# Rounding work given to GpSimd and weight loads to SyncE's queue, in a two-layer model on eight cores

## The chip, the cores and the metric

The kernel runs on all 8 cores of one Trainium2 chip. Each core computes one sequence of a batch of 8, with all weights; the cores exchange nothing. The metric is the device time of the slowest core, in microseconds (us).

## The reference

Two layers with layer norms behind every block, on x of [8, 2048, 1024]. Cut to what matters:

```python
# layer 0
x = _layernorm(x + _L0_attn_ref(x, ...))   # k, v, sigmoid(r); a scan over time; Wo
x = _layernorm(x + _L0_ffn_ref(x, ...))    # 1024 -> 4096 -> 4096 -> 4096 -> 1024
# layer 1: every linear layer is quantized
x = _layernorm(x + _L1_attn_ref(x, ...))
x = _layernorm(x + _L1_ffn_ref(x, ...))    # 1024 -> 4096, conv over 3 tokens, silu, 4096 -> 1024

def act_quant(x):       # per token
    scale = 127.0 / clip(max(abs(x), axis=-1), 1e-05)
    return clip(round(x * scale), -128.0, 127.0) / scale
def weight_quant(w):    # per matrix
    scale = 1.0 / clip(mean(abs(w)), 1e-05)
    return clip(round(w * scale), -1.0, 1.0) / scale
def bitlinear(x, norm_w, w, b=None):
    return act_quant(rmsnorm(x, norm_w)) @ weight_quant(w).T
def _L1_attn_ref(x, ...):
    q, k, v, g = bitlinear(x, nq, wq), ...            # 1024, 1024, 2048, 2048 wide
    gk = log_sigmoid(bitlinear(bitlinear(x, ngk1, wgk1), ngk2, wgk2, bgk2)) / 16
    # S = exp(gk_t) S + k_t v_t ; o_t = q_t S, per head, over time
    return bitlinear(o * silu(g), no, wo)
```

## The kernel before

Five engines run in parallel: TensorE (PE, "t" in the code), VectorE (DVE, "v"), ScalarE (ACT, "s"), GpSimd (POOL, "g") and SyncE (SP, "y"). `Prog` keeps one list of instructions for each. `P.op(engine, fn, after=...)` appends a computation that waits on the semaphores of the tokens in `after`, its own engine's too; `P.dma(queue, out, in_, after=..., new=True)` appends a DMA to the list of the engine that issues it. Each engine executes its list strictly in order. So an instruction's place in the program decides what it stands behind, and a DMA issued by POOL stands behind all that POOL has to do before it.

The work goes through eight stages on activations XA that stay in SBUF: first attention, LN 1, first feed-forward, LN 2, layer 1's attention, LN 3, layer 1's feed-forward, LN 4.

**Weight prepass** (`_emit_prepass`). Layer 1's nine weight matrices are made ternary beforehand and written to DRAM. A matrix is cut in tiles of 128x1024 fp32 (512 KB): 137 tiles in all, 32 of them of f1T, 32 of f2T, 16 of owT. Every tile passes twice. In `t_red` it is loaded, ACT sums its absolute values into `red` (L393), and POOL adds that to `acc` (L397). After the matrix's last tile comes its scale: a matmul on PE (L403) and an op on DVE (L406). In `t_quant` it is loaded again, DVE turns it to -1, 0 or 1 in three ops (L425, L428, L431: v1, v2, v4), and POOL stores it, in eight DMAs for a tile of f1T or f2T and one for the others. These pieces (301 in all) stand in a list `P.bg`. `P.pump(1)` calls in the first attention (96) and in LN 1 (16) put one each between the stage's instructions, and `P.pump_all()` after LN 1 puts all the rest there, before the first feed-forward.

**Layer 1's attention** (`stage_l1attn`) runs over 8 blocks of 256 tokens. In a block X2 holds two token tiles (tt) of 128 x 1024. For each of the five projections in NPROJ (q, k, v, g, gk1) and each of the two tiles, DVE multiplies by the norm vector NB (p1, L973), takes the maximum (p2, L977), computes four columns of scales in `CL` (p3 to p6), and rounds in seven ops q1 to q7 (L991 to L1005): scale, cast to int32, cast back, difference, two comparisons that correct the rounding, and unscale. The tensors are QSz, QSi, QSt, QSd. PE transposes the tile in eight matmuls (L1014) into banks 5 and 6, DVE evacuates them into XQF (L1019), and the projection's matmuls (L1057 or L1076) read XQF and the weights WL, a single buffer of 2 MB that a DMA on POOL's queue fills. Then a chunked scan over time (L1157 to L1262) yields OG for each of two halves `cn` of the block. OG is quantized in two halves of 1024 (L1311 to L1324, y1 to y8, eight ops each, the same kind as p1 and q1 to q7), transposed, and multiplied with owT, which comes in two loads (`rnd`) into WL.

**Layer 1's feed-forward** (`stage_l1ffn`) runs over four quarters of 512 tokens. Each of four token tiles is transposed, copied to QZ, scaled and rounded by seven ops like q1 to q7 (L1499 to L1508), and transposed back into XQ3. 32 output slices with f1T follow, then the convolution, then `_act_quant_fm` (L1386 to L1409), which rounds HC (128 x 16384) in 16 pieces of 1024, eight ops each, then 8 slices with f2T. Weights come through three buffers FWJ on POOL's queue, each load after the matmuls that read its buffer last.

In both stages one token `vt` threads all of DVE's ops.

## Time and profile before

| | us |
|---|---|
| median of 3 runs | 12935.47 (12914.56 to 12952.62) |
| the profiled execution, its own time | 12926.71 |
| its span, first to last instruction, on the slowest core | 12925.1 |
| spans of the 8 cores | 12856.7 to 12925.1 |
| busy: PE, weight loads, DVE | 5345.3, 2561.2, 3718.3 |
| busy: ACT, POOL | 1284.4, 908.4 |

The profiled execution's time is 8.8 us below the median and 1.6 us above its own span. A stage by stage table of the trace is the way to read this profile, since no engine is busy throughout: the whole-span shares mix stages with different limits. The first attention ends near 890 us, LN 1 near 1,126, the drained prepass near 2,510, the first feed-forward near 6,915, LN 2 near 7,075, layer 1's attention near 10,600, LN 3 near 10,756, layer 1's feed-forward near 12,770. Of POOL's instructions nearly all are DMA issues; the rest are adds and memsets of one column.

### The profile page before, as it was taken

Reading aid. Unit: us, or ns where it says so; the run is one execution under the profiler, and the core shown is the slowest. Engines: PE = TensorE matmul, PEld = TensorE weight load, DVE = VectorE, ACT = ScalarE, POOL = GpSimd, SP = SyncE. Lnnn points to the kernel's source line nnn. Section 1 sums busy time; section 2 is a strip of 40 time slices with the busy share of each in tenths; the row PEclk is TensorE's granted clock in tenths of the full one; section 3 lists DMA queues with packets and bytes.
Section 4 is the critical chain, followed back from the end, with each engine's and each line's share of the span. In section 5 each row is a group of like instructions: output and inputs, shape, how many; then the busy total and the mean of one; then the engine's idle time right before and its main releaser. Section 6 shows DMA issues by size and latency. Waiting matters only on the chain.

```text
span 12925.1 us, 71867 instructions; the slowest of 8 cores (12856.7 to 12925.1 us)
## 1 busy us (share of the span) xinstructions
PE 5345.3 (41%) x22678; PEld 2561.2 (20%) x22678; DVE 3718.3 (29%) x6428; ACT 1284.4 (10%) x2046; POOL 908.4 (7%) x1789
## 2 busy tenths in 40 slices
PE   2431000166666666666664333333333333324323
PEld 0110000022222222222222222222221222111111
DVE  5752120210000001000002444444444434553553
ACT  1221101010000001000002100100010012011011
POOL 1011142300000000000000000000000000000000
PEclk7665555588888887888886666666666666657656
DMA  4221222222222222222221111111111101001002
GB/s 102 63 75 58 83 65 77 60 39 44 43 43 43 44 39 40 43 43 43 46 43 27 55 56 55 42 56 56 42 41 56 69 20 32 24 29 52 24 29 73
DMA packets 169413, 637.25 MB, mean 49 GB/s; under 512 B 28928, under 2 KB 29568, under 8 KB 157776
## 3 DMA queue, kind: packets, MB, share of 16 engines
q0 software_dynamic: 163136, 615.49, 18.5%
q1 hardware_dynamic: 5904, 17.17, 0.4%
q8 instruction: 187, 3.06, 0.1%
q14 instruction: 186, 1.52, 0.0%
HBM read 794.50 MB, written 42.01 MB: 65 GB/s over the span
## 4 chain that ended last, share of the span: by engine, by line
PE 37%; DVE 25%; DMA 20%; issue 8%; ACT 5%; POOL 3%; DVEq 1%; another core or an unknown queue 0%; ACTq 0%; POOLq 0%; SPq 0%
PE ps L817 16%; PE ps L769 5%; DMA f_wj<-h1R 4%; DMA f_wj<-h2R 4%; PE ps L1634 2%; DMA pre_in<-f1T 2%; PE ps L854 2%; DMA pre_in<-f2T 2%; DMA f_wj<-w1R 2%; PE ps L1076 2%; PE ps L1241 2%; PE ps L1534 2%; PE ps L1357 1%; PE ps L1057 1%; DMA b_wj<-q_f2T 1%
## 5 line engine op out<-in xcount | busy, mean ns | idle before, releaser
L817 PE MATMUL ps<-f_h,f_wj 128*128 128x512 bf16 x8192 | 2014.2, 412 | 1103.2 <-DMA f_wj<-h1R 554.3
L817 PEld LDWEIGHTS ps<-f_h,f_wj 128*128 128x128 bf16 x8192 | 855.2, 104 | 2262.3 <-issue 1471.8
L865 DVE SCALAR_TENSOR_TENSOR XA<-ps,SVEC,XA 128x512 f32<-128x512 f32 x32 | 24.0, 751 | 3478.8 <-PE ps L854 3477.1
L769 PE MATMUL ps<-f_h,f_wj 128*128 128x512 bf16 x2048 | 584.8, 456 | 690.1 <-DMA f_wj<-w1R 683.1
L1634 PE MATMUL ps<-b_hc,b_wj 128*128 128x512 bf16 x1024 | 280.1, 442 | 607.9 <-DVE b_hc L1406 466.5
L403 PE MATMUL ps<-pre_acc,c_ones 128*128 128x1 f32 x18 | 4.7, 332 | 1201.2 <-POOL pre_acc L397 1201.2
L828 ACT ACTIVATE f_h<-ps,f_sc 128x512 bf16<-128x512 f32 x256 | 175.9, 687 | 2893.6 <-PE ps L817 2881.4
L769 PEld LDWEIGHTS ps<-f_h,f_wj 128*128 128x128 bf16 x2048 | 232.0, 113 | 1042.4 <-issue 897.4
L1014 PE MATMUL ps<-c_idb,a_qz 128*128 128x128 bf16 x640 | 77.7, 298 | 766.6 <-DVE a_qz L1005 766.6
L1076 PE MATMUL ps<-a_wl,a_xqf 128*128 128x512 bf16 x1024 | 302.8, 468 | 149.9 <-DMA a_wl<-q_vwT 68.0
L789 DVE SCALAR_TENSOR_TENSOR f_h<-ps,f_sc,f_g 128x512 bf16<-128x512 f32 x128 | 96.1, 751 | 796.8 <-ACT f_g L779 790.1
L425 DVE TENSOR_SCALAR pre_in<-pre_in,pre_rs 128x1024 f32<-128x1024 f32 (+1 forms) x137 | 98.9, 722 | 771.3 <-DMA pre_in<-f1T 287.4
L854 PE MATMUL ps<-f_h,f_wj 128*128 128x512 bf16 x1024 | 251.6, 412 | 136.8 <-DMA f_wj<-w3R 136.8
L1221 PE MATMUL ps<-a_qg,a_kp 128*128 128x128 f32 x256 | 76.4, 454 | 524.9 <-DVE a_kg L1214 524.9
L1579 PE MATMUL ps<-c_idb,b_hc 128*128 128x128 bf16 x512 | 74.9, 301 | 523.9 <-ACT b_hc L1562 396.8
L393 ACT ACTIVATE pre_in<-pre_in 128x1024 f32<-128x1024 f32 (+1 forms) x137 | 138.0, 1007 | 1358.9 <-DMA pre_in<-f2T 544.0
L1634 PEld LDWEIGHTS ps<-b_hc,b_wj 128*128 128x128 bf16 x1024 | 111.0, 111 | 781.3 <-issue 698.8
L1534 PE MATMUL ps<-b_xq,b_wj 128*128 128x512 bf16 x1024 | 240.8, 387 | 15.8 <-DMA b_wj<-q_f1T 8.3
L403 PEld LDWEIGHTS ps<-pre_acc,c_ones 128*128 128x128 f32 x18 | 4.4, 298 | 1203.3 <-issue 1203.2
L1357 PE MATMUL ps<-a_oqf,a_wl 128*128 128x128 bf16 x2048 | 179.1, 273 | 152.6 <-DMA a_wl<-q_owT 139.0
L529 PE MATMUL ps<-l_xk,l_wk 128*128 128x512 bf16 x256 | 106.5, 591 | 324.5 <-DVE l_xr L515 183.0
L687 PE MATMUL ps<-c_idf,ln_tm 128*128 128x128 f32 x384 | 93.1, 423 | 310.7 <-DVE ln_tm L668 310.7
(323 smaller groups left out, 7916.2 us busy)
## 6 DMA issues: line engine op xcount, KB each, us to landing
f_wj<-h1R POOLq DMA_DIRECT2D x128, 512.0 KB, 6.4
f_wj<-h2R POOLq DMA_DIRECT2D x128, 512.0 KB, 6.2
a_wl<-q_owT POOLq DMA_DIRECT2D x32, 2048.0 KB, 7.8
b_wj<-q_f2T POOLq DMA_DIRECT2D x80, 512.0 KB, 4.6
pre_in<-f1T POOLq DMA_DIRECT2D x64, 512.0 KB, 3.9
pre_in<-f2T POOLq DMA_DIRECT2D x64, 512.0 KB, 3.8
a_wl<-q_vwT POOLq DMA_DIRECT2D x16, 2048.0 KB, 7.6
a_wl<-q_gwT POOLq DMA_DIRECT2D x16, 2048.0 KB, 7.6
```

The lines of the kernel that those rows point to most:

```text
L393: s1 = P.op("s", lambda s: s.activation(buf[0:rr, 0:cc], buf[0:rr, 0:cc], AF.Abs, accum_out=pre["red"][0:rr, :]), after=[ld, state["s"], s ...
L529: mmK = P.op("t", lambda t, c=c, i=i, bk=bk: t.matmul(PS[bk][:, :], WK[:, i, c * 128:(c + 1) * 128], XK[:, i, :], start=(i == 0), stop=(i ...
L769: t.matmul(PS[bank][:, :], wb[:, i, :], XB[:, i, s2 * 512:(s2 + 1) * 512], start=(i == 0), stop=(i == NC - 1)),
L817: off=off, SRC=SRC: t.matmul(PS[bank][:, :], wb[:, i2, :], SRC[:, i * 1024 + off:i * 1024 + off + 512], start=(i == 0), stop=(i == 31)),
L828: DST=DST: s.activation(DST[:, j * 1024 + off:j * 1024 + off + 512], PS[bank][:, :], AF.Gelu, scale=SC[:, scoff + j:scoff + j + 1]),
L854: off=off: t.matmul(PS[bank][:, :], wb[:, i2, :], H0[:, i * 1024 + off:i * 1024 + off + 512], start=(i == 0), stop=(i == 31)),
L1057: mm = P.op("t", lambda t, i=i, j=j, bank=bank: t.matmul(PS[bank][:, 0:256], WLv[:, i, j * 128:(j + 1) * 128], XQF[:, i, :], start=(i == 0 ...
L1076: t.matmul(PS[bank][:, :], XQF[:, i, tt * 128:(tt + 1) * 128], WLv[:, i, ds * 512:(ds + 1) * 512], start=(i == 0), stop=(i == NC - 1)),
L1241: omm = P.op("t", lambda t, h=h, j=j: t.matmul(PS[3][:, :], QG[:, j, :], S[:, 2 * h + j, :], start=(j == 0), stop=False), after=[f3, bank_ ...
L1357: cc=cc: t.matmul(PS[bank][:, cc * 128:(cc + 1) * 128], WLv[:, i, jj * 128:(jj + 1) * 128], OQF[:, rnd * 8 + i, :], start=(rnd == 0 and i ...
L1534: mm = P.op("t", lambda t, slot=slot, i=i, j=j, bank=bank: t.matmul(PS[bank][:, :], FWJ[slot][:, i, :], XQ3[:, i, :], start=(i == 0), stop ...
L1634: t.matmul(PS[bank][:, :], FWJ[s_][:, i2, :], HC[:, i, :], start=(i == 0), stop=(i == 31)),
```

## The change

There are two parts.

1. In the prepass, loads are issued by SP instead of POOL, into three buffers instead of two. A reduce load waits for the ACT op that read its buffer three tiles ago, no longer for POOL's last add; `red` has two buffers. A quantize load waits for the DVE op that read its buffer three tiles ago and for `state["v"]`; the wait for the earlier store moves from the load to v4. The scale's matmul uses bank 7 instead of 6.
2. In layer 1, part of the rounding runs on POOL. In the attention: of every projection the second token tile (p1, q1 to q7, not p2 to p6), and of the output quantization the second half (y1 to y8). In the feed-forward: of four token tiles the second and fourth, and of `_act_quant_fm`'s pieces every second. POOL has buffers of its own (Q2z, Q2i, Q2t, Q2d, CL2, MSKF) and its own token `gt`. Rounding goes through a new helper, `_round_fix`: on DVE five ops as before, on POOL seven, since each scalar_tensor_tensor becomes a comparison and an add. `zb_free` makes the writer of a buffer wait for the transposes that read it. The norm vector's load waits for both tiles' p1, no longer for the end of the block before.

```diff
-                buf = (pre["in0"], pre["in1"])[ti % 2]
-                ld = P.dma("g", buf[0:rr, 0:cc], src[r0:r0 + rr, c0:c0 + cc],
-                           after=[state["g"]], new=True)
+                buf = pre["ins"][ti % NR]
+                red = pre["reds"][ti % 2]
+                ld = P.dma("y", buf[0:rr, 0:cc], src[r0:r0 + rr, c0:c0 + cc],
+                           after=[state["ld"][ti % NR]], new=True)
                 s1 = P.op("s", lambda s: s.activation(
                     buf[0:rr, 0:cc], buf[0:rr, 0:cc], AF.Abs,
-                    accum_out=pre["red"][0:rr, :]), after=[ld, state["s"], state["g"]])
+                    accum_out=red[0:rr, :]), after=[ld, state["s"],
+                                                    state["redf"][ti % 2]])
                 state["s"] = s1
+                state["ld"][ti % NR] = s1
                 state["g"] = P.op("g", lambda g: g.tensor_add(
-                    pre["acc"][0:rr, :], pre["acc"][0:rr, :], pre["red"][0:rr, :]),
+                    pre["acc"][0:rr, :], pre["acc"][0:rr, :], red[0:rr, :]),
                     after=[s1, state["g"]])
+                state["redf"][ti % 2] = state["g"]
...
-                buf = (pre["in0"], pre["in1"])[ti % 2]
-                obuf = (pre["out0"], pre["out1"])[ti % 2]
-                ld = P.dma("g", buf[0:rr, 0:cc], src[r0:r0 + rr, c0:c0 + cc],
-                           after=[state["qd"][ti % 2], state["v"], state["g"]], new=True)
+                buf = pre["ins"][ti % NR]
+                obuf = pre["outs"][ti % 2]
+                ld = P.dma("y", buf[0:rr, 0:cc], src[r0:r0 + rr, c0:c0 + cc],
+                           after=[state["ld"][ti % NR], state["v"]], new=True)
                 v1 = P.op("v", lambda v: v.tensor_single_scalar(
                     buf[0:rr, 0:cc], buf[0:rr, 0:cc], pre["rs"][0:rr, :], ALU.mult),
                     after=[ld, state["v"]])
@@ -430,8 +436,9 @@
                     ALU.is_le, ALU.mult), after=[v1])
                 v4 = P.op("v", lambda v: v.scalar_tensor_tensor(
                     obuf[0:rr, 0:cc], buf[0:rr, 0:cc], 0.5, pre["cmp"][0:rr, 0:cc],
-                    ALU.is_ge, ALU.add), after=[v2])
+                    ALU.is_ge, ALU.add), after=[v2, state["qd"][ti % 2]])
                 state["v"] = v4
+                state["ld"][ti % NR] = v4
...
                 d_nb = P.dma("g", NB[:, 0:1024], din[nnm], new=True,
-                             after=[nb_free])
+                             after=[nb_free2[0], nb_free2[1]])
                 qtoks = []
                 for tt in range(2):
-                    p1 = P.op("v", lambda v, tt=tt: v.tensor_mul(
-                        QSz[:], X2[:, tt, :], NB[:, 0:1024]),
-                        after=[d_nb, x2tok, vt])
-                    nb_free = p1
-                    p2 = P.op("v", lambda v: v.reduce_max(
-                        CL[:, 4:5], QSz[:], axis=AXX, apply_absolute_value=True),
-                        after=[p1])
-                    p3 = P.op("v", lambda v, tt=tt: v.tensor_scalar(
-                        CL[:, 5:6], CL[:, 4:5], CL[:, tt:tt + 1], 1e-5,
+                    en = "v" if tt == 0 else "g"
+                    Zb, Ib, Tb, Db = (QSz, QSi, QSt, QSd) if tt == 0 else (Q2z, Q2i, Q2t, Q2d)
+                    CLx = CL if tt == 0 else CL2
+                    ch = vt if tt == 0 else gt
+                    p1 = P.op(en, lambda v, tt=tt, Zb=Zb: v.tensor_mul(
+                        Zb[:], X2[:, tt, :], NB[:, 0:1024]),
+                        after=[d_nb, x2tok, ch, zb_free[tt]])
+                    nb_free2[tt] = p1
+                    p2 = P.op("v", lambda v, Zb=Zb, CLx=CLx: v.reduce_max(
+                        CLx[:, 4:5], Zb[:], axis=AXX, apply_absolute_value=True),
+                        after=[p1, vt])
+                    p3 = P.op("v", lambda v, tt=tt, CLx=CLx: v.tensor_scalar(
+                        CLx[:, 5:6], CLx[:, 4:5], CL[:, tt:tt + 1], 1e-5,
                         ALU.mult, ALU.max), after=[p2, c3])
-                    p4 = P.op("v", lambda v: v.reciprocal(CL[:, 6:7], CL[:, 5:6]),
-                              after=[p3])
-                    p5 = P.op("v", lambda v, tt=tt: v.scalar_tensor_tensor(
-                        CL[:, 7:8], CL[:, 6:7], 127.0, CL[:, tt:tt + 1],
+                    p4 = P.op("v", lambda v, CLx=CLx: v.reciprocal(
+                        CLx[:, 6:7], CLx[:, 5:6]), after=[p3])
+                    p5 = P.op("v", lambda v, tt=tt, CLx=CLx: v.scalar_tensor_tensor(
+                        CLx[:, 7:8], CLx[:, 6:7], 127.0, CL[:, tt:tt + 1],
                         ALU.mult, ALU.mult), after=[p4])
-                    p6 = P.op("v", lambda v: v.tensor_scalar(
-                        CL[:, 8:9], CL[:, 5:6], 1.0 / 127, None, ALU.mult),
+                    p6 = P.op("v", lambda v, CLx=CLx: v.tensor_scalar(
+                        CLx[:, 8:9], CLx[:, 5:6], 1.0 / 127, None, ALU.mult),
                         after=[p5])
-                    q1 = P.op("v", lambda v: v.tensor_single_scalar(
-                        QSz[:], QSz[:], CL[:, 7:8], ALU.mult), after=[p6])
-                    q2 = P.op("v", lambda v: v.tensor_copy(QSi[:], QSz[:]),
-                              after=[q1])
-                    q3 = P.op("v", lambda v: v.tensor_copy(QSt[:], QSi[:]),
-                              after=[q2])
-                    q4 = P.op("v", lambda v: v.tensor_sub(QSd[:], QSz[:], QSt[:]),
-                              after=[q3])
-                    q5 = P.op("v", lambda v: v.scalar_tensor_tensor(
-                        QSt[:], QSd[:], 0.5, QSt[:], ALU.is_ge, ALU.add),
-                        after=[q4])
-                    q6 = P.op("v", lambda v: v.scalar_tensor_tensor(
-                        QSt[:], QSd[:], -0.5, QSt[:], ALU.is_gt, ALU.add),
-                        after=[q5])
-                    q7 = P.op("v", lambda v: v.tensor_scalar(
-                        QSz[:], QSt[:], 1.0, CL[:, 8:9], ALU.subtract, ALU.mult),
+                    if tt == 0:
+                        vt = p6
+                    q1 = P.op(en, lambda v, Zb=Zb, CLx=CLx: v.tensor_single_scalar(
+                        Zb[:], Zb[:], CLx[:, 7:8], ALU.mult), after=[p6, ch])
+                    q6 = _round_fix(P, en, Zb, Ib, Tb, Db, Zb, q1)
+                    q7 = P.op(en, lambda v, Zb=Zb, Tb=Tb, CLx=CLx: v.tensor_scalar(
+                        Zb[:], Tb[:], 1.0, CLx[:, 8:9], ALU.subtract, ALU.mult),
                         after=[q6])
-                    vt = q7
+                    if tt == 0:
+                        vt = q7
+                    else:
+                        gt = q7
                     xtp = []
                     for c in range(NC):
                         bank = 5 + c // 4
                         cc = c % 4
                         a = [q7, bank_free[bank]] if (c % 4 == 0) else []
-                        xtp.append(P.op("t", lambda t, c=c, bank=bank, cc=cc: t.transpose(
+                        xtp.append(P.op("t", lambda t, c=c, bank=bank, cc=cc, Zb=Zb:
+                                        t.transpose(
                             PSB[bank][:, cc * 128:(cc + 1) * 128],
-                            QSz[:, c * 128:(c + 1) * 128], IDB[:]), after=a))
+                            Zb[:, c * 128:(c + 1) * 128], IDB[:]), after=a))
+                    zb_free[tt] = xtp[-1]
...
+                    en = "v" if half == 0 else "g"
+                    Zb, Ib, Tb, Db = (QSz, QSi, QSt, QSd) if half == 0 else (Q2z, Q2i, Q2t, Q2d)
+                    ch = vt if half == 0 else gt
+                    y1 = P.op(en, lambda v, half=half, Zb=Zb: v.tensor_mul(
+                        Zb[:], OG[:, half * 1024:(half + 1) * 1024],
+                        NOB[:, half * 1024:(half + 1) * 1024]),
+                        after=[ch, w7, zb_free[half]])
+                    y2 = P.op(en, lambda v, Zb=Zb: v.tensor_single_scalar(
+                        Zb[:], Zb[:], CL[:, 7:8], ALU.mult), after=[y1])
+                    y7_ = _round_fix(P, en, Zb, Ib, Tb, Db, Zb, y2)
+                    y8 = P.op(en, lambda v, Zb=Zb, Tb=Tb: v.tensor_scalar(
+                        Zb[:], Tb[:], 1.0, CL[:, 8:9], ALU.subtract, ALU.mult),
+                        after=[y7_])
+                    ytoks[half] = y8
+                    if half == 0:
+                        vt = y8
+                    else:
+                        gt = y8
...
+def _round_fix(P, en, Zb, Ib, Tb, Db, M, prev):
+    o1 = P.op(en, lambda v, Zb=Zb, Ib=Ib: v.tensor_copy(Ib[:], Zb[:]), after=[prev])
+    o2 = P.op(en, lambda v, Ib=Ib, Tb=Tb: v.tensor_copy(Tb[:], Ib[:]), after=[o1])
+    o3 = P.op(en, lambda v, Zb=Zb, Tb=Tb, Db=Db: v.tensor_sub(Db[:], Zb[:], Tb[:]),
+              after=[o2])
+    if en == "v":
+        o4 = P.op(en, lambda v, Tb=Tb, Db=Db: v.scalar_tensor_tensor(
+            Tb[:], Db[:], 0.5, Tb[:], ALU.is_ge, ALU.add), after=[o3])
+        o5 = P.op(en, lambda v, Tb=Tb, Db=Db: v.scalar_tensor_tensor(
+            Tb[:], Db[:], -0.5, Tb[:], ALU.is_gt, ALU.add), after=[o4])
+    else:
+        o4a = P.op(en, lambda v, Db=Db, M=M: v.tensor_single_scalar(
+            M[:], Db[:], 0.5, ALU.is_ge), after=[o3])
+        o4 = P.op(en, lambda v, Tb=Tb, M=M: v.tensor_add(Tb[:], Tb[:], M[:]),
+                  after=[o4a])
+        o5a = P.op(en, lambda v, Db=Db, M=M: v.tensor_single_scalar(
+            M[:], Db[:], -0.5, ALU.is_gt), after=[o4])
+        o5 = P.op(en, lambda v, Tb=Tb, M=M: v.tensor_add(Tb[:], Tb[:], M[:]),
+                  after=[o5a])
+    return o5
+
+
+def _act_quant_fm(P, flat, UB, WB, QSV, QSG, vt, gt, ready=None):
     piece = 1024
     for pc in range(16384 // piece):
         o0 = pc * piece
-        q1 = P.op("v", lambda v, o0=o0: v.tensor_mul(
+        en = "v" if pc % 2 == 0 else "g"
+        QI, QT, QD, QM = QSV if pc % 2 == 0 else QSG
+        ch = vt if pc % 2 == 0 else gt
+        q1 = P.op(en, lambda v, o0=o0: v.tensor_mul(
             flat[:, o0:o0 + piece], flat[:, o0:o0 + piece], UB[:, 0:piece]),
-            after=[vt])
-        q2 = P.op("v", lambda v, o0=o0: v.tensor_copy(
-            QI[:, 0:piece], flat[:, o0:o0 + piece]), after=[q1])
-        q3 = P.op("v", lambda v: v.tensor_copy(QT[:, 0:piece], QI[:, 0:piece]),
-                  after=[q2])
-        q4 = P.op("v", lambda v, o0=o0: v.tensor_sub(
-            QD[:, 0:piece], flat[:, o0:o0 + piece], QT[:, 0:piece]), after=[q3])
-        q5 = P.op("v", lambda v: v.scalar_tensor_tensor(
-            QT[:, 0:piece], QD[:, 0:piece], 0.5, QT[:, 0:piece], ALU.is_ge, ALU.add),
-            after=[q4])
-        q6 = P.op("v", lambda v: v.scalar_tensor_tensor(
-            QT[:, 0:piece], QD[:, 0:piece], -0.5, QT[:, 0:piece], ALU.is_gt, ALU.add),
-            after=[q5])
-        q7 = P.op("v", lambda v: v.tensor_scalar(
+            after=[ch, ready if pc < 2 else None])
+        q6 = _round_fix(P, en, flat[:, o0:o0 + piece], QI[:, 0:piece],
+                        QT[:, 0:piece], QD[:, 0:piece], QM[:, 0:piece], q1)
+        q7 = P.op(en, lambda v, QT=QT: v.tensor_scalar(
             QT[:, 0:piece], QT[:, 0:piece], 1.0, None, ALU.subtract), after=[q6])
-        q8 = P.op("v", lambda v, o0=o0: v.tensor_mul(
+        q8 = P.op(en, lambda v, o0=o0, QT=QT: v.tensor_mul(
             flat[:, o0:o0 + piece], QT[:, 0:piece], WB[:, 0:piece]), after=[q7])
-        vt = q8
-    return vt
+        if pc % 2 == 0:
+            vt = q8
+        else:
+            gt = q8
+    return vt, gt
...
+                en = "v" if tt % 2 == 0 else "g"
+                Zb, Ib, Tb, Db = (QZ, QI, QT, QD) if tt % 2 == 0 else (Q2z, Q2i, Q2t, Q2d)
+                CLx = CL if tt % 2 == 0 else CL2
+                ch = vt if tt % 2 == 0 else gt
...
+                b1 = P.op(en, lambda v, Zb=Zb, CLx=CLx: v.tensor_single_scalar(
+                    Zb[:], Zb[:], CLx[:, 3:4], ALU.mult), after=[a5, ch])
+                b6 = _round_fix(P, en, Zb, Ib, Tb, Db, MSKF[tt % 2], b1)
+                b7 = P.op(en, lambda v, Zb=Zb, Tb=Tb, CLx=CLx: v.tensor_scalar(
+                    Zb[:], Tb[:], 1.0, CLx[:, 4:5], ALU.subtract, ALU.mult), after=[b6])
+                if tt % 2 == 0:
+                    vt = b7
+                else:
+                    gt = b7
...
+            vt, gt = _act_quant_fm(P, HC[:, :, :].rearrange("p c n -> p (c n)"),
+                                   UB, WB, (QI, QT, QD, MSKF[0]),
+                                   (Q2i, Q2t, Q2d, MSKF[1]), vt, gt, ready=vt)
+            hq_tok = (vt, gt)
```

## Rows read from the trace of the kernel before

**Rows 1.** The page, 40 slices: busy tenths of PE.
```profile
PE   2431000166666666666664333333333333324323
```

**Rows 2.** Busy time by stretch: two of the prepass, layer 1's attention and feed-forward.
```profile
core 0: us, PE busy (x) PEld busy (x) DVE busy (x) ACT busy (x) POOL busy (x), PEclk, DMA share, GB/s
1348.00:1548.00 200.00, 0.00 (x0) 0.00 (x0) 0.00 (x0) 35.88 (x63) 24.48 (x65) 0.50 0.28 85
1548.00:1932.00 384.00, 0.56 (x2) 0.50 (x2) 85.86 (x98) 0.90 (x2) 150.09 (x283) 0.50 0.22 65
7075.00:10600.00 3525.00, 1301.94 (x6359) 767.50 (x6357) 1641.02 (x3157) 323.20 (x548) 66.42 (x124) 0.64 0.15 51
10756.00:12770.00 2014.00, 666.22 (x2857) 290.98 (x2856) 953.94 (x1516) 181.72 (x257) 103.17 (x194) 0.64 0.11 34
```

**Rows 3.** Timeline, start and us: one reduce tile of f1T.
```profile
1512.10 0.57 POOL L81 DMA_DIRECT2D pre_in<-f1T  x1 [0.62 <-POOL pre_acc L397]
1516.12 1.06 ACT L393 ACTIVATE pre_in<-pre_in 128x1024 f32<-128x1024 f32 x1 [4.97 <-DMA pre_in<-f1T]
...
1518.22 0.57 POOL L81 DMA_DIRECT2D pre_in<-f1T  x1 [0.62 <-POOL pre_acc L397]
```

**Rows 4.** Timeline: one quantize tile of f1T, from v4 to v4.
```profile
1844.63 1.23 DVE L431 SCALAR_TENSOR_TENSOR pre_out<-pre_in,pre_cmp 128x1024 bf16<-128x1024 f32 x1
1846.39 4.26 POOL L81 DMA_DIRECT2D q_f1T<-pre_out  x8 [6.97 <-DVE pre_out L431]
1850.64 0.54 POOL L81 DMA_DIRECT2D pre_in<-f1T  x1
1854.70 0.75 DVE L425 TENSOR_SCALAR pre_in<-pre_in,pre_rs 128x1024 f32<-128x1024 f32 x1 [8.84 <-DMA pre_in<-f1T]
...
1856.36 1.23 DVE L431 SCALAR_TENSOR_TENSOR pre_out<-pre_in,pre_cmp 128x1024 bf16<-128x1024 f32 x1
```

**Rows 5.** Groups: busy, mean ns | idle before, releaser; DVE, 88 to 1,126 us.
```profile
L542 DVE TENSOR_TENSOR l_ekv<-l_ek,ps 128x512 f32<-128x512 f32 x32 | 21.9, 684 | 50.6 <-ACT l_ek L533 47.9 <-PE ps L538 1.7
...
L406 DVE TENSOR_SCALAR SCL<-ps 128x1 f32<-128x1 f32 x6 | 0.9, 156 | 73.7 <-PE ps L403 73.7
```

**Rows 6.** Timeline: q's second tile q1, q7, matmuls; k's weight load.
```profile
7098.13 0.49 DVE L991 TENSOR_SCALAR a_qz<-a_qz,a_cl 128x1024 bf16<-128x1024 bf16 x1
...
7103.77 0.49 DVE L1005 TENSOR_SCALAR a_qz<-a_qt,a_cl 128x1024 bf16<-128x1024 bf16 x1
...
7106.26 9.56 PE L1057 MATMUL ps<-a_xqf,a_wl 128*128 128x256 bf16 x64 [0.85 <-DVE a_xqf L1019]
...
7116.42 0.53 POOL L81 DMA_DIRECT2D a_wl<-q_kwT  x1 [19.70 <-PE ps L1057]
```

**Rows 7.** Timeline of DVE: output quantization, first y1, y2, and the last y8.
```profile
7362.89 0.69 DVE L1311 TENSOR_TENSOR a_qz<-a_og,a_nob 128x1024 bf16<-128x1024 bf16 x1
7363.69 0.48 DVE L1314 TENSOR_SCALAR a_qz<-a_qz,a_cl 128x1024 bf16<-128x1024 bf16 x1
...
7378.23 0.49 DVE L1324 TENSOR_SCALAR a_qz<-a_qt,a_cl 128x1024 bf16<-128x1024 bf16 x1
```

**Rows 8.** Groups by form: DVE's two-input op, the scan, POOL's add.
```profile
L1002 DVE SCALAR_TENSOR_TENSOR a_qt<-a_qd,a_qt 128x1024 bf16<-128x1024 bf16 x80 | 98.0, 1225 | 8.7 <-DVE a_qt L999 0.5
...
L562 DVE TENSOR_TENSOR_SCAN l_A<-SVEC,l_A,l_ekv 128x512 f32<-128x512 f32 x32 | 41.1, 1285 | 3.7 <-DVE l_B L560 0.5
...
L397 POOL TENSOR_TENSOR pre_acc<-pre_acc,pre_red 128x1 f32<-128x1 f32 x136 | 28.2, 207 | 763.8 <-ACT pre_in L393 763.8
```

**Rows 9.** DMA issues: count, KB each, median us from issue to landing.
```profile
a_wl<-q_owT POOLq DMA_DIRECT2D x32, 2048.0 KB, 7.8
b_wj<-q_f2T POOLq DMA_DIRECT2D x80, 512.0 KB, 4.6
...
out<-ln_tm SPq DMA_DIRECT2D x16, 512.0 KB, 2.7
```

**Rows 10.** The page's groups: f2T's matmuls and what they wait for.
```profile
L1634 PE MATMUL ps<-b_hc,b_wj 128*128 128x512 bf16 x1024 | 280.1, 442 | 607.9 <-DVE b_hc L1406 466.5
```

More of the change, by code:

```diff
@@ L928, in stage_l1attn @@
         vt = vz2
+        gt = None
+        nb_free2 = [None, None]
+        zb_free = [None, None]
         stt = None
@@ L1328, in stage_l1attn @@
                     otp = []
+                    Zb2 = QSz if half == 0 else Q2z
                     for c in range(NC):
@@ L1442, in stage_l1ffn @@
         vt = o1
+        gt = None
         stt = None
+        zb_free = [None, None]
         wj_free = [None, None, None]
```

117 lines of the change are left out of this document (51 added, 66 removed).

## The prediction

> **What bounds the kernel now.** I read the slices first. PE idles from about 1,290 to 2,260 us [rows 1], and the table by stage says what runs there. Two stretches matter: one where ACT works for 36 us in 200 and DVE not at all, and one where POOL issues DMAs for 150 us in 384 while DVE works for 86 [rows 2]. This is the weight prepass, drained before the first feed-forward: nothing is saturated, each tile is a chain. The third place is layer 1. In its attention, 3,525 us long, DVE is busy 1,641 and PE 1,302; in its feed-forward, 2,014 us long, 954 and 666; POOL has 66 and 103 [rows 2]. PE and DVE take turns there. In the first feed-forward, between them, the code is not touched.
>
> **Prepass, reduce tiles.** A tile costs 6.1 us now: issue on POOL, ACT 4.0 us later, then POOL's add, then 0.62 us until the next issue, which waits for the add [rows 3]. Afterwards the load waits only for the ACT three tiles back. A ring of three gives (4.0 + 1.25 + 0.1 of semaphore)/3 = 1.8 us; ACT alone needs 1.06 + 0.19 = 1.25 (its second instruction reads the accumulator, 0.19). The transfer rate sets a floor near that: 2 MB arrive in about 7.8 us [rows 9], so 0.5 MB need 1.95. I take 1.9. In the drain are 16 + 32 + 32 = 80 such tiles (owT, f1T, f2T): 80 x (6.15 - 1.9) = **-340**. Bounds: 1.25 (-390), and no overlap on SP's queue, 5.3 (-65).
>
> **Prepass, quantize tiles.** The new load still waits for the previous tile's last DVE op, since state["v"] is in its list. So it does not pipeline; it only no longer stands behind POOL's stores. Now 11.73 us from one v4 to the next: v4, the eight stores 4.26, the load 4.05, DVE 1.66 until v4 [rows 4]. After: v4 end to load 0.5, landing 4.05, three DVE ops 2.9: 7.4. The stores (0.5 + 4.3) fit below it. 64 tiles x 4.4 = **-282**. If a load on SP lands like the 512 KB output there, 2.7 [rows 9], 6.0 and -365; if POOL's stores collide with DVE, as slow as 9 and -175. owT has one store per tile: 8.3 now, by the same count, so 16 x 0.9 = **-14**; the small gk1/gk2 tiles **-10**.
>
> **Prepass under the first attention and LN.** 112 of the 301 pieces run there. DVE waits 73.7 us for scales that hang on the POOL chain and 47.9 for an exp behind ACT's reductions [rows 5]. I take **-70**; bounds 0 and -122. Prepass together: **-716**.
>
> **What a POOL operation costs.** The trace has no wide POOL arithmetic. The chain of seven DVE ops (q1 to q7) becomes nine on POOL, because _round_fix splits each scalar_tensor_tensor in two; the eight-op chains become ten. Let P be one such op with its gap to the next (each waits for its own engine's semaphore). From below: DVE's own chain, 7098.13 to 7104.26, 6.13/7 = 0.88 [rows 6]. From above: the slowest streaming row, the scan, 1.285 us for 512, so 2.57 for 1,024, plus POOL's 0.62 gap: 3.2 [rows 3, 8]. Nearest, I think, is DVE without a fast mode, 1.225 for 1,024, times the ratio that a 128x1 op shows, 207 ns on POOL to 156 on DVE: 1.63 [rows 5, 8]. For the gap I take 0.3, between DVE's 0.11 [rows 7] and 0.62. **P = 1.9**.
>
> The Trainium skill, "GPSIMD Engine Reference", sections 3.1 and 4.1, has a two-input fp32 add of 2,048 at 4,497 ns on GpSimd and 2,293 on DVE, and one-input ops near line rate of a 1.2 GHz clock. An estimate from it: 2.25 and 0.85 us for 1,024, so with gaps 14.6 us for nine ops and 17 to 18.5 for ten. By that the whole sum would be about +130, not +298. No row here shows either.
>
> **Attention projections, 8 blocks x 5 = 40.** The intent to overlap fails on DVE's order: the second tile's reduce_max, p3 to p6 stand behind the first tile's q7 and its two evacuations, and after q1 to q7 of the second tile DVE's next instruction is that tile's evacuation, which waits for POOL. Only p1 (0.69 + 0.1) runs beside the first tile. Each: 9 x 1.9 - 6.13 - 0.8 = +10.2 [rows 6]; **+407**.
>
> **What queues behind POOL.** All weight loads of this stage are issued by POOL. Now the load for k goes out at 7116.42, as soon as q's matmuls end, and lands behind the quantization. After, it stands behind q7 of the second tile. It lands 7.8 us after issue (the row is owT's, same 2 MB) [rows 6, 9]; the matmuls could start 2.0 us after q7 (7104.26 to 7106.26) [rows 6]. With 0.3 to issue: 6.1 us bare, for q, k, and the first halves of v and g: 32 x 6.1 = **+195**. The norm-vector loads are also behind, but DVE needs them only after the matmuls: nothing. The output projection's first load is prefetched during the scan now; it will stand behind POOL's half: 16 x 6.1 = **+98**.
>
> **Output quantization, 16 times.** Here the halves do overlap. Now 15.8 us from y1 to the end of the second y8 [rows 7]; after, POOL's ten ops 19.0: +3.2, **+51**. Attention together +751.
>
> **Feed-forward.** Two of four token tiles per quarter: 8 x (17.1 - 6.1) = **+88**. _act_quant_fm: PE waits 466.5/4 = 116.6 us per quarter for it [rows 10], 16 pieces of 7.2. After, DVE's eight take 58 and POOL's eight 8 x 10 x 1.9 = 152; 4 x 36 = **+146**. f2T's first two loads now stand behind it: 1.1 + 4.6 [rows 9], 4 x 5.7 = **+23**; f1T's first, smaller, hides but for 1.5: **+6**. Together +263. Extra tiles and zb_free waits: for work long done, nothing; the evacuation hides them.
>
> **The sum.** -716 + 751 + 263 = +298 on the profiled execution's 12,926.7: 13,225. It lies 9 us below the median; I forecast **13,230**. The count of moved operations is 360 + 160 + 72 + 320, of which all are exposed: 912 us for each us of P. Even is P = 1.9 - 298/912 = 1.57.
>
> **Rivals.**
> - *POOL is nearly as fast as DVE.* One mechanism: P under 1.57, everywhere. At 1.3 the chains cost 547 less: 12,680. For it: 128x1 ops differ by a third only, and DVE's fast modes reach 0.69. Against: more instructions, each with a semaphore. The kernel gets **faster**. 0.18.
> - *The two engines block each other where they do overlap.* In _act_quant_fm DVE's 58 us would add to POOL's: 4 x 58 = 230; in the output quantization 16 x 7.0 = 112; POOL's p1 beside the first tile 40 x 1.6 = 64. Up to +406: 13,630. Nothing in the trace speaks of it, since POOL had no wide op. The Trainium skill, "SBUF — State Buffer", "Who interferes with whom", says just this: the port pair is locked for a whole instruction, by DVE ops with two SBUF inputs or in a two-port mode. 0.17. A P of 2.3 would land at the same place (+365); 0.08 more.
> - *SP's loads do not overlap.* Reduce tiles at 5.3: +275, 13,500. The three buffers and the different queue speak against. 0.07.
> - The forecast, P between 1.57 and 2.2 and both gains of the prepass: 0.5. Its own range 12,930 to 13,500.
>
> **How the numbers follow.** A measurement tells about 0.3% (39 us) from no change. P's bounds from rows alone would give 12,300 to 14,400. The range leaves out one in ten on each side: at the low end P = 1.5 with a prepass gain near its bound, 12,850; at the high end most of the lock, 13,700. Faster 0.18, same 0.05 (P within 0.04 of 1.57), slower 0.77.
>
> **What would show it.** Reduce tiles 1.9 us apart and quantize tiles 7.4, feed-forward starting near 1,800 instead of 2,510. POOL rows of 128x1024 at 1.6 us. PE waiting for POOL's a_q2z; DMA a_wl<-q_qwT, q_kwT new among its releasers; attention 4,280 us long instead of 3,525, feed-forward 2,280. Wrong if POOL's ops are near 1.2, if the weights still land in time, or if the prepass saves much more than 720.

## The result, and the profile after

The changed kernel takes 13,734.8 us (median of 8 runs, 13,719.7 to 13,763.9) beside 12,916.8 us before: a ratio of 1.063, 95% interval 1.0617 to 1.0643. It is **slower by 818 us**; I had forecast 13,230, and my range ended at 13,700. Between the profiled executions the spans differ by 13,736.8 - 12,925.1 = 811.7 us. In some executions, more of them in the later experiments, the cores of one die or of both show a lower granted clock and take some per cent longer, so for those experiments I also give the spans of the undisturbed cores.

**Busy time by stretch, kernel after.** The first four are f1T's reduce and quantize tiles, then f2T's; the last two are layer 1's attention and feed-forward, the stretches of [rows 2].

```profile
core 6: us, PE busy (x) PEld busy (x) DVE busy (x) ACT busy (x) POOL busy (x), PEclk, DMA share, GB/s
1142.00:1218.00 76.00, 0.00 (x0) 0.00 (x0) 0.00 (x0) 36.76 (x64) 5.92 (x31) 0.50 0.76 225
1218.00:1456.00 238.00, 0.56 (x2) 0.50 (x2) 83.94 (x95) 0.00 (x0) 132.11 (x243) 0.50 0.34 102
1456.00:1530.00 74.00, 0.00 (x0) 0.00 (x0) 2.67 (x3) 36.76 (x64) 13.89 (x48) 0.50 0.74 241
1530.00:1748.00 218.00, 0.56 (x2) 0.50 (x2) 86.64 (x99) 0.00 (x0) 147.56 (x248) 0.50 0.36 115
6332.00:10942.00 4610.00, 1297.35 (x6355) 766.81 (x6353) 1366.07 (x2710) 323.01 (x548) 1384.80 (x683) 0.61 0.11 39
11098.00:13613.00 2515.00, 668.93 (x2988) 295.54 (x2988) 915.70 (x1224) 181.85 (x258) 1004.54 (x595) 0.62 0.09 29
```

Two signs matter. In the prepass, ACT's 36 us of reductions now fill 76 us instead of 200. In layer 1, PE does the same work in over 1,000 us more of attention; DVE gave up 275 us of work there, and POOL took on 1,318 us for it. The granted clock of that stretch is 0.61 on average instead of 0.64, while PE is busy 28% of it instead of 37%. PE's busy time is the same, 1,297 and 1,302 us, so a slower PE is no part of the loss.

By landmarks: the first feed-forward starts at 1,747.7 instead of 2,508.2 us, and layer 1's attention at 6,335.6 instead of 7,079.1, **-744** (17 of the first 761 are given back in the first feed-forward and LN 2, where the diff changes nothing). From the attention's first op to its last the time is 4,600.2 instead of 3,515.2, **+1,085**. What is left is the last feed-forward with its layer norms, **+470**. The sum is +811.

**Timeline, kernel after: POOL's chain for q's second tile, and what waits for it** (start, us; the whole chain is shown, since its prices decide this case; the last row holds the 22 of 64 matmuls that the window takes in).

```profile
6355.27 2.85 POOL L1011 TENSOR_SCALAR a_q2z<-a_q2z,a_cl 128x1024 bf16<-128x1024 bf16 x1 [13.80 <-DVE a_cl L1006]
6358.27 1.04 POOL L1406 CAST a_q2i<-a_q2z 128x1024 int32<-128x1024 bf16 x1 [0.15 <-POOL a_q2z L1011]
6359.44 1.04 POOL L1407 CAST a_q2t<-a_q2i 128x1024 bf16<-128x1024 int32 x1
6360.63 2.12 POOL L1408 TENSOR_TENSOR a_q2d<-a_q2z,a_q2t 128x1024 bf16<-128x1024 bf16 x1 [0.15 <-POOL a_q2t L1407]
6362.92 2.77 POOL L1416 TENSOR_SCALAR a_q2z<-a_q2d 128x1024 bf16<-128x1024 bf16 x1 [0.17 <-POOL a_q2d L1408]
6365.84 2.12 POOL L1418 TENSOR_TENSOR a_q2t<-a_q2t,a_q2z 128x1024 bf16<-128x1024 bf16 x1
6368.11 2.78 POOL L1420 TENSOR_SCALAR a_q2z<-a_q2d 128x1024 bf16<-128x1024 bf16 x1 [0.16 <-POOL a_q2t L1418]
6371.04 2.12 POOL L1422 TENSOR_TENSOR a_q2t<-a_q2t,a_q2z 128x1024 bf16<-128x1024 bf16 x1
6373.34 3.71 POOL L1014 TENSOR_SCALAR a_q2z<-a_q2t,a_cl 128x1024 bf16<-128x1024 bf16 x1 [0.18 <-POOL a_q2t L1422]
6377.00 0.67 POOL L81 DMA_DIRECT2D a_wl<-q_qwT  x1
...
6377.99 0.95 DVE L1033 COPY a_xqf<-ps 128x512 bf16<-128x512 bf16 x2 [22.92 <-PE ps L1027]
...
6385.40 4.85 PE L1071 MATMUL ps<-a_xqf,a_wl 128*128 128x256 bf16 x22 [7.08 <-DMA a_wl<-q_qwT]
```

The chain takes 6355.27 to 6377.05, 21.8 us, where DVE's seven ops took 6.13 [rows 6]. DVE stands idle behind it for 22.9 us: its next instruction is the evacuation. POOL issues the weight load only then, and PE starts 8.35 us after q7 instead of 2.0 [rows 6].

**The page's groups, kernel after: what PE waits for.**

```profile
L1685 PE MATMUL ps<-b_hc,b_wj 128*128 128x512 bf16 x1024 | 277.1, 438 | 952.8 <-DMA b_wj<-q_f2T 952.8
L1027 PE MATMUL ps<-c_idb,a_q2z 128*128 128x128 bf16 x320 | 40.5, 307 | 1016.9 <-POOL a_q2z L1014 1016.9
L1378 PE MATMUL ps<-a_oqf,a_wl 128*128 128x128 bf16 x2048 | 181.2, 274 | 247.3 <-DMA a_wl<-q_owT 247.3
```

1,016.9 us over 40 chains are 25.4 each: the chain and what precedes it. The first row answers to [rows 10]. Its releaser is now a DMA, but that load was issued 4.6 us before it landed, behind POOL's last piece. Most of the 952.8 us is POOL's arithmetic, as e3 shows below.

### The profile page after: what moved, and what is told of

It reads as the page before. It is cut to its first block, busy times and chain, and to the rows that moved or that the text cites. A ratio compares the mean times of both kernels' runs of the same rounds, so it can differ in the third digit from the quotient of the medians.

```text
span 13736.8 us, 72786 instructions; the slowest of 8 cores (13698.5 to 13736.8 us)
## 1 busy us (share of the span) xinstructions
PE 5344.5 (39%) x22678; PEld 2560.7 (19%) x22678; DVE 3401.9 (25%) x5668; ACT 1283.9 (9%) x2046; POOL 2991.6 (22%) x2467
## 3 DMA queue, kind: packets, MB, share of 16 engines
q14 instruction: 192, 1.57, 0.0%
## 4 chain that ended last, share of the span: by engine, by line
PE 35%; DMA 20%; DVE 17%; POOL 15%; issue 8%; ACT 4%; DVEq 1%; POOLq 0%; ACTq 0%; SPq 0%
PE ps L824 15%; PE ps L776 4%; DMA f_wj<-h1R 3%; DMA f_wj<-h2R 3%; PE ps L1685 2%; PE ps L861 2%; DMA a_wl<-q_owT 2%; DMA f_wj<-w1R 2%; PE ps L1090 2%; PE ps L1257 2%; DMA pre_in<-f1T 1%; PE ps L1584 1%; PE ps L1378 1%; DMA b_wj<-q_f2T 1%; DMA pre_in<-f2T 1%
## 5 line engine op out<-in xcount | busy, mean ns | idle before, releaser
L1685 PE MATMUL ps<-b_hc,b_wj 128*128 128x512 bf16 x1024 | 277.1, 438 | 952.8 <-DMA b_wj<-q_f2T 952.8
L1027 PE MATMUL ps<-c_idb,a_q2z 128*128 128x128 bf16 x320 | 40.5, 307 | 1016.9 <-POOL a_q2z L1014 1016.9
L1090 PE MATMUL ps<-a_wl,a_xqf 128*128 128x512 bf16 x1024 | 296.0, 459 | 255.0 <-DMA a_wl<-q_gwT 127.4
L81 POOL DMA_DIRECT2D f_wj<-h2R x128 | 67.5, 532 | 1500.9 <-PE ps L824 1495.4
L81 POOL DMA_DIRECT2D f_wj<-h1R x128 | 67.5, 532 | 1489.0 <-PE ps L824 1458.7
L1331 POOL TENSOR_TENSOR a_q2z<-a_og,a_nob 128x1024 bf16<-128x1024 bf16 x16 | 41.4, 2589 | 1498.9 <-DVE a_cl L1323 1498.9
L1033 DVE COPY a_xqf<-ps 128x512 bf16<-128x512 bf16 x160 | 67.9, 425 | 959.1 <-PE ps L1027 950.9
L1378 PE MATMUL ps<-a_oqf,a_wl 128*128 128x128 bf16 x2048 | 181.2, 274 | 247.3 <-DMA a_wl<-q_owT 247.3
L1011 POOL TENSOR_SCALAR a_q2z<-a_q2z,a_cl 128x1024 bf16<-128x1024 bf16 x40 | 113.8, 2844 | 704.1 <-DVE a_cl L1006 704.1
```

What stands on the lines that cost most here:

```text
L81: return eng.dma_start(out=out, in_=in_)
L1011: q1 = P.op(en, lambda v, Zb=Zb, CLx=CLx: v.tensor_single_scalar(Zb[:], Zb[:], CLx[:, 7:8], ALU.mult), after=[p6, ch])
L1090: t.matmul(PS[bank][:, :], XQF[:, i, tt * 128:(tt + 1) * 128], WLv[:, i, ds * 512:(ds + 1) * 512], start=(i == 0), stop=(i == NC - 1)),
L1378: cc=cc: t.matmul(PS[bank][:, cc * 128:(cc + 1) * 128], WLv[:, i, jj * 128:(jj + 1) * 128], OQF[:, rnd * 8 + i, :], start=(rnd == 0 and i ...
L1685: t.matmul(PS[bank][:, :], FWJ[s_][:, i2, :], HC[:, i, :], start=(i == 0), stop=(i == 31)),
```

## The experiments

The theory behind all of them is that a POOL op costs about 2.3 us or more with its gap to the next, and that its chains are exposed, which means that nothing else runs meanwhile. What each run tests, and its rival, stands in its expectation. The diffs are against the kernel after, unless another is named.

**e1_prepass_only and e2_layer1_only.** Each keeps one half of the diff and sets the other back to the kernel before: e1 keeps the prepass half, e2 the layer 1 half. A piece of e1's edit:

```diff
-                    en = "v" if tt == 0 else "g"
-                    Zb, Ib, Tb, Db = (QSz, QSi, QSt, QSd) if tt == 0 else (Q2z, Q2i, Q2t, Q2d)
...
+                    p1 = P.op("v", lambda v, tt=tt: v.tensor_mul(
+                        QSz[:], X2[:, tt, :], NB[:, 0:1024]),
```

> Only the prepass part of the change (loads on SP, three buffers), layer 1 as before. Theory A: the two parts add, and the changed kernel's trace already shows the prepass part's worth, since layer 1's attention starts about 744 us earlier: 12,917 - 744 = 12,170 us. Rival B: part of the early start is paid back in later stages that the same edit disturbs (the first feed-forward's loads, clock), and this kernel lands at 12,300 or above. The prediction's own term was -716.

> Only the layer 1 part (rounding on POOL), the prepass as before. Theory A, additive: 12,917 + 1,085 in the attention + 470 in the feed-forward = 14,470 us. If the two parts help each other (rival B), the sum of both differences does not give the changed kernel's +818, and this run is below 14,400 or above 14,550. The prediction's terms gave +1,014: 13,930.

e1 took 12,194.2 us, ratio 0.941 (0.937 to 0.945): -745. e2 took 14,519.2, ratio 1.123 (1.117 to 1.129): +1,580. The parts add up: -745 + 1,580 = +835, and +818 was measured for both; the difference is inside e2's interval of some 70 us. The prepass half is a gain by itself; the loss is layer 1's alone.

**e6_pool_prices.** A kernel of its own that computes nothing of the reference and writes zeros. It runs ops of 128x1024 on POOL alone, six in a row of each kind, and then beside DVE. In outline, one kind alone and one pair:

```diff
+        for _ in range(6):
+            g = P.op("g", lambda e: e.tensor_single_scalar(GB[:], GB2[:], 0.5, ALU.is_ge), after=[g])
...
+        pair(lambda e: e.tensor_add(GB[:], GB2[:], GB2[:]),
+             lambda e: e.tensor_mul(VB[:], VB2[:], VB3[:]), 12, 30)
```

> A kernel of its own that computes nothing of the reference (it writes zeros): POOL operations of 128x1024 alone, six of each form, then five pairs in which POOL and DVE run chains side by side. From the changed kernel's trace: comparison with a constant bf16 2.77 us, with a column 2.84, two ops 3.71, add of two tensors 2.12, cast 1.04. Theory A: tensor_scalar is slow on POOL in itself (2.8 here too, alone), and fp32 operands change little. Theory B: the 2.8 comes from neighbours (DVE holding the port) and alone it is about 1.0 like the cast. For the pairs: if the engines block each other, a DVE multiply of two bf16 tensors rises from 0.69 us towards 2 us or more beside POOL's adds, a reduce_max of one tensor stays at 1.22; if they do not, all keep their prices.

Groups by form of this kernel; first POOL alone:

```profile
L202 POOL TENSOR_SCALAR g_b<-g_b 128x1024 bf16<-128x1024 bf16 x6 | 16.6, 2768 | 0.9 <-POOL g_b L202 0.8 <-POOL g_c L195 0.2
L208 POOL TENSOR_SCALAR g_f<-g_f 128x1024 f32<-128x1024 f32 x6 | 16.6, 2768 | 0.9 <-POOL g_f L208 0.8 <-POOL g_f L206 0.2
L212 POOL TENSOR_SCALAR g_b<-g_b,g_c 128x1024 bf16<-128x1024 bf16 x6 | 22.2, 3704 | 1.0 <-POOL g_b L212 0.9 <-POOL g_b L210 0.2
L222 POOL CAST g_i<-g_b 128x1024 int32<-128x1024 bf16 x6 | 6.2, 1040 | 0.8
L224 POOL TENSOR_SCALAR g_b<-g_b 128x512 bf16<-128x512 bf16 x6 | 8.9, 1488 | 0.9 <-POOL g_b L224 0.8 <-POOL g_i L222 0.2
```

Then the pairs, each DVE row above the POOL row that ran beside it:

```profile
L236 DVE TENSOR_TENSOR v_b<-v_b 128x1024 bf16<-128x1024 bf16 x30 | 38.8, 1293 | 3.5 <-DVE v_b L236 0.5
L235 POOL TENSOR_TENSOR g_b<-g_b 128x1024 bf16<-128x1024 bf16 x12 | 26.1, 2173 | 1.7
...
L242 DVE TENSOR_REDUCE v_c<-v_b 128x1 f32<-128x1024 bf16 x20 | 24.4, 1220 | 2.1
L241 POOL TENSOR_TENSOR g_b<-g_b 128x1024 bf16<-128x1024 bf16 x12 | 22.7, 1892 | 1.7
...
L244 DVE SCALAR_TENSOR_TENSOR v_b<-v_b 128x1024 bf16<-128x1024 bf16 x20 | 42.5, 2126 | 2.1
L243 POOL TENSOR_TENSOR g_b<-g_b 128x1024 bf16<-128x1024 bf16 x12 | 32.5, 2707 | 1.7
```

On POOL alone a tensor_scalar with a constant costs 2.77 us, a comparison like a product and bf16 like fp32; with a column of scales it costs 2.84, and with two operations 3.70. A copy or cast costs 1.04. A tensor_tensor costs 1.89 here, with the same tensor as both inputs, and 2.12 in the kernel, where the inputs differ (no run separates that from other causes). With gaps of 0.15 to 0.17 the prices of this kernel give 21.1 us for the nine ops, and with 2.12 for the three tensor_tensor 21.8, as seen. So POOL's own price is enough to explain the chain, without any contention. The pairs show contention too: DVE's product takes 1.29 us on average where it takes 0.69 alone [rows 7], and its scalar_tensor_tensor 2.13 where it takes 1.225 [rows 8], while POOL's partner slows from 1.89 to 2.71. These are means over all of DVE's ops, some of which ran when POOL was done; beside POOL a product took 2.2 us at most. In the two pairs that are not shown, DVE's difference took 0.91 beside POOL's comparison (2.89 instead of 2.77), and its tensor_scalar 1.06 instead of 0.49 beside POOL's add (1.92). The reduce, one input in and one column out, keeps its 1.22 us, and its partner its 1.89.

**e3_loads_on_sp.** All weight loads of layer 1 go to SP's queue; the arithmetic stays on POOL.

```diff
-                    d_w = P.dma("g", WLv[:, :, :], wq[:, half, :, :],
+                    d_w = P.dma("y", WLv[:, :, :], wq[:, half, :, :],
...
-            tok = P.dma("g", dst, s_, after=[wj_free[slot]] + list(after), new=True)
+            tok = P.dma("y", dst, s_, after=[wj_free[slot]] + list(after), new=True)
```

> The changed kernel with layer 1's weight loads (WL for q, k, v, g and the output projection, and the three FWJ buffers) issued by SP instead of POOL; the norm vector's load stays on POOL. Theory: 48 loads of 2 MB stand bare behind POOL's rounding at 6 to 6.5 us each, and 8 smaller ones cost 29 us in all: 13,735 - 300 - 29 = 13,400 us. Rival: the loads are hidden anyway or limited by the transfer and not by where they are queued: 13,650 to 13,735.

13,395.4 us, ratio 1.033 (1.027 to 1.039), where 13,400 was expected. Four of PE's waits shrink: for q's and k's matmuls (L1071) from 112.9 to 12.8, for v's and g's (L1090) from 255.0 to 143.5, for the output projection (L1378) from 247.3 to 138.3, for f2T's (below) from 952.8 to 909.2; together -364. The medians of the two dies' spans are 13,341 and 13,375 against 13,708 and 13,712 after, some -350, of which I had +322 in the sum (195 + 98 + 23 + 6); that they stood behind POOL's arithmetic is shown. In the page's groups of this kernel f2T's matmuls now wait for POOL's last product, where the kernel after named a DMA; the wait for the second tile is unchanged, since the arithmetic is:

```profile
L1685 PE MATMUL ps<-b_hc,b_wj 128*128 128x512 bf16 x1024 | 291.5, 455 | 909.2 <-POOL b_hc L1441 786.9
L1027 PE MATMUL ps<-c_idb,a_q2z 128*128 128x128 bf16 x320 | 40.5, 305 | 1018.1 <-POOL a_q2z L1014 1018.1
```

**e8_no_correction.** POOL's four ops that correct the rounding are left out (so its half is rounded as the cast does it), with everything else as after.

```diff
-        o4a = P.op(en, lambda v, Db=Db, M=M: v.tensor_single_scalar(
-            M[:], Db[:], 0.5, ALU.is_ge), after=[o3])
...
+        o5 = o3
```

> The changed kernel without the correction of the rounding on POOL: the two comparisons and two adds of _round_fix are left out there (DVE keeps its own). Theory: every microsecond of POOL's chains is one of the kernel. Left out are 2 x (2.77 + 2.12) + 4 x 0.15 = 10.4 us in each of 40 + 16 + 8 chains and 32 pieces: 96 x 10.4 = -1,000, so 12,740 us. Rival: something else (the loads behind POOL, or DVE's own order) ends last once POOL is shorter, and the time stays above 13,000.

A single run: 12,831.4 us. Its undisturbed cores lie at 12,713 to 12,741, against 13,699 to 13,737 in the profile of the kernel after, and 13,740 to 13,780 for the same kernel in e10. That is some -990 by the first and -1,030 by the second. The four ops cost 2 x 2.92 + 2 x 2.27 = 10.4 us with gaps, and 40 + 16 + 8 + 32 = 96 chains of them give 998. PE's wait for the second tile's q7 fell from 1,016.9 to 601.1, by 10.4 for each of 40:

```profile
L1027 PE MATMUL ps<-c_idb,a_q2z 128*128 128x128 bf16 x320 | 40.5, 306 | 601.1 <-POOL a_q2z L1014 601.1
```

A microsecond of POOL's chain is a microsecond of the kernel.

**e5_scales_first, repeated as e5b_scales_first beside e10_changed_again** (the kernel after, unaltered). p1 to p6 of both tiles go ahead of the first tile's q1, so POOL can quantize beside DVE.

```diff
-                    if tt == 0:
-                        vt = p6
+                    p6s[tt] = p6
+                    vt = p6
+                for tt in range(2):
...
-                        Zb[:], Zb[:], CLx[:, 7:8], ALU.mult), after=[p6, ch])
+                        Zb[:], Zb[:], CLx[:, 7:8], ALU.mult), after=[p6s[tt], ch])
```

> The changed kernel with one order altered: in a projection, p1 to p6 of both token tiles come first, then q1 to q7 of the first on DVE and of the second on POOL. Theory: POOL's 21.8 us chain is bare in the changed kernel only because p2 to p6 stand behind DVE's first tile; started before it, it hides that tile's rounding and evacuation (6.1 + 2.0 us), less p2 waiting for POOL's p1 (1.4 us) and what the two block in each other: 40 x 5 to 7 us = -200 to -280, so 13,455 to 13,535 (changed kernel: 13,735). Rival: POOL and DVE block each other so much that nothing is won: 13,700 or above.

> The same kernel as e5_scales_first, once more beside the changed kernel on one chip, since the first gave no clean ratio. Theory as before: 200 to 280 us under the changed kernel; its undisturbed cores showed 13,495 to 13,538. Rival: no difference.

> The changed kernel unaltered, as the yardstick on the same chip for the three others: 13,700 to 13,760 us.

e5 gave 13,699 us without a ratio; its undisturbed cores lie at 13,440 to 13,454. e5b gave 13,623.6, ratio 1.048 (1.040 to 1.056). e10 gave 13,865.2, above the expected 13,700 to 13,760, but with a ratio of 1.067 (1.057 to 1.078) and undisturbed cores at 13,696 to 13,715, which repeats the result. The two ratios differ by 0.0195, 252 us, with wide intervals; the undisturbed cores of e5b, 13,449 to 13,492, lie some 230 lower than e10's. That is inside the expected 200 to 280, and the groups of PE's matmuls in e5b give the same:

```profile
L1033 PE MATMUL ps<-c_idb,a_q2z 128*128 128x128 bf16 x320 | 40.5, 306 | 613.7 <-POOL a_q2z L1020 613.7
L1033 PE MATMUL ps<-c_idb,a_qz 128*128 128x128 bf16 x320 | 40.5, 306 | 539.3 <-DVE a_qz L1020 539.3
```

In e10 the two waits are 1,016.6 and 365.8. The second tile gains 403 and the first, whose chain now stands behind the other's p1 and scales, loses 173: net -229. DVE's order was a cause, but the smaller one: the projections' part of the loss is +596 (below).

**e4_split_12_4.** The prepass of e1, and in _act_quant_fm every fourth piece on POOL, the others on DVE; the rest of layer 1 is all DVE. By prices alone, POOL's four pieces (4 x 22.5 = 90 us) would end 4 us after DVE's twelve (86) and 25 before DVE's sixteen of e1 (115).

```diff
-        en = "v" if pc % 2 == 0 else "g"
+        en = "g" if pc % 4 == 1 else "v"
```

> The prepass part, and of the layer 1 part only this: in _act_quant_fm every fourth piece runs on POOL, twelve on DVE; the projections, the output quantization and the feed-forward's token tiles are rounded on DVE alone. Beside the kernel with the prepass part alone (12,194 us). If the engines did not disturb each other, DVE's 12 x 7.2 = 86 us and POOL's 4 x 24.2 = 97 us would end 18 us per quarter before DVE's 115 alone: 12,194 - 70 = 12,120. Theory: with POOL's operation in progress DVE's are held for its length, so DVE slows to POOL's rhythm while POOL runs and the split gives nothing or loses: 12,190 to 12,300.

12,254.9 us, ratio 0.941 (0.936 to 0.947), as e1's 0.941; undisturbed cores 12,162 to 12,191 against e1's 12,110 to 12,127. Nothing is gained, some 50 us are lost, as the theory said. PE's wait for DVE's b_hc is 551.0 in total; the second row is e1's:

```profile
L1675 PE MATMUL ps<-b_hc,b_wj 128*128 128x512 bf16 x1000 | 288.9, 456 | 693.7 <-DVE b_hc L1434 551.0 <-DMA b_wj<-q_f2T 140.7 <-issue 1.1
...
L1641 PE MATMUL ps<-b_hc,b_wj 128*128 128x512 bf16 x1024 | 279.7, 441 | 611.7 <-DVE b_hc L1413 469.3 <-DMA b_wj<-q_f2T 142.3
```

With the work shared 12 to 4 DVE got later by 20 us a quarter: in the trace its twelve pieces take 135.4 us, where sixteen take 115.4 in e1, and POOL's four take 104 to 107.

**e7_loads_ahead, repeated as e7b_loads_ahead.** e1, with the previous tile's last DVE op taken off the quantize load's list; the three buffers are guarded by state["ld"] as in e1. The diff is against e1.

```diff
-                           after=[state["ld"][ti % NR], state["v"]], new=True)
+                           after=[state["ld"][ti % NR]], new=True)
```

> The prepass part alone, with one wait removed: a quantize load no longer waits for state[v], only for the DVE op that used its buffer three tiles ago. Theory: that wait is why quantize tiles stay at about 7.4 us; without it the load hides and the eight stores on POOL (4.3 us plus a hand-over of 0.5) are next: 64 x 2.6 = -166, owT's 16 at 2.9 instead of 7.4, -70: about 11,960. Rival: the stores, which cannot be issued while DVE runs fp32 ops in a fast mode, take the place of the load's wait and tiles stay above 6.5: 12,100 or more.

> The prepass part with loads ahead, once more: undisturbed cores had 11,836 to 11,899, so 11,860 to 11,930 us and a ratio near 0.92.

12,133 us, ratio 0.919 (0.910 to 0.928), undisturbed cores 11,836 to 11,899, below the expected 11,960; e7b 12,037.6, with no ratio, its cores at 11,841 to 11,889. The first feed-forward starts at 1,474.6 instead of 1,738.9 in e1: -264. Timeline of DVE in e7, v4 of successive f2T tiles:

```profile
1387.99 1.23 DVE L437 SCALAR_TENSOR_TENSOR pre_out<-pre_in,pre_cmp 128x1024 bf16<-128x1024 f32 x1 [3.56 <-DMA q_f2T<-pre_out]
...
1393.80 1.22 DVE L437 SCALAR_TENSOR_TENSOR pre_out<-pre_in,pre_cmp 128x1024 bf16<-128x1024 f32 x1 [2.93 <-DMA q_f2T<-pre_out]
...
1399.01 1.23 DVE L437 SCALAR_TENSOR_TENSOR pre_out<-pre_in,pre_cmp 128x1024 bf16<-128x1024 f32 x1 [2.33 <-DMA q_f2T<-pre_out]
```

These three are 5.8 and 5.2 us apart; over all of f2T (1325.8 to 1473.2) and f1T the mean is 4.8 and 4.9 us, where e1 has 6.9 and 7.1. The wait has moved from the load to POOL's stores, whose issue of eight takes 4.3 [rows 4]. The 64 tiles give 137 us. The rest of the 264 is mostly owT's tiles, at 3.4 instead of 7.1 us, and the first attention, which ends 48 us earlier.

**e9_ahead_and_sp.** e7 with e3's edit.

> e7_loads_ahead with layer 1's weight loads on SP as well. POOL computes nothing in layer 1 here. Theory: moving the loads paid 340 us in e3 only because POOL's rounding stood before them; here it should pay at most the shorter landing, 7.4 instead of 7.8 us for the 32 loads that are bare anyway and as little for the small ones: -10 to -40. Rival: SP's queue is better in itself, -150 or more.

11,972.2 us, ratio 0.917 (0.893 to 0.942); undisturbed cores 11,793 to 11,838, some 30 to 50 below e7 and e7b. Without arithmetic on POOL the queue of the loads hardly matters. e7 and e9 beat both kernels, by about 8% on before.

## Why the prediction went wrong, step by step

**The step that failed is P, "1.9 us for one POOL op with its gap".** It was scaled from DVE's 1.225 by the ratio of two 128x1 ops, and such ops are nearly all fixed cost: POOL's took 0.21 us. On POOL a 128x512 tensor_scalar takes 1.49 us and a 128x1024 one 2.77; by these two sizes that is 0.2 fixed and 2.5 ns for each element of a row. The mean over the projections' nine ops is 21.8/9 = 2.42, over the output quantization's ten 24.1/10 = 2.41, over _act_quant_fm's ten 22.5/10 = 2.25; over all 912 moved operations 2.36. That is inside my bounds of 0.88 and 3.2, and above the 2.2 that the forecast's own case allowed. The mechanism, exposed chains and weight loads behind them, was right; the size of P was not. And P alone would not have left the range: 13,225 + 912 x 0.46 is some 13,640. The second term that I had at nothing in the sum, the two engines blocking each other, adds 103 and takes it past 13,700. I had priced "P of 2.3" (0.08) and the blocking (0.17) as rivals that land at the same place; both came at once. My signs of being wrong named a cheap POOL, but not a dear one.

The Trainium skill, "GPSIMD Engine Reference", section 3.1, would make a two-input op of this size 2.25 us by an estimate from its 4,497 ns; the trace is near, with 2.12. By its section 4.1 one-input ops run roughly at line rate, 0.85 by the prediction's estimate; casts are near that with 1.04, but tensor_scalar took 2.77 and 3.70, and the measurement decides.

**The blocking is real, and smaller than its price in the rival.** _act_quant_fm in the kernel after, timeline of POOL's first op of a piece, beside DVE and then alone:

```profile
11464.01 2.91 POOL L1434 TENSOR_TENSOR b_hc<-b_hc,b_ub 128x1024 bf16<-128x1024 bf16 x1
...
11490.35 2.91 POOL L1434 TENSOR_TENSOR b_hc<-b_hc,b_ub 128x1024 bf16<-128x1024 bf16 x1
...
11562.70 2.12 POOL L1434 TENSOR_TENSOR b_hc<-b_hc,b_ub 128x1024 bf16<-128x1024 bf16 x1
...
11585.16 2.12 POOL L1434 TENSOR_TENSOR b_hc<-b_hc,b_ub 128x1024 bf16<-128x1024 bf16 x1
```

A piece takes POOL 26.3 us beside DVE and 22.5 alone. POOL's eight take 194.8 in that quarter, where eight alone would be 179.7: 15 a quarter, **+60**. In the output quantization POOL's ten ops take 26.8 us (6722.88 to 6749.64); by their prices alone, the 21.8 of the nine and a product of 2.12 with its gap, they would take 24.1: 16 x 2.7 = **+43**. DVE suffers more: its eight pieces of 7.2 us last from 11412.63 to 11521.3, 109 us instead of 58. But DVE waits for POOL anyway, so that costs nothing here. It does where DVE is the bound, as e4 showed. I had priced this rival at up to +406 by adding DVE's whole time to POOL's; both are slowed, and each by part. The Trainium skill, "SBUF — State Buffer", "Who interferes with whom", has the lock for DVE ops with two inputs in SBUF or in a two-port mode, and none for a reduce; e6 agrees, with the reduce at 1.22 us untouched.

**Term by term.**

- *Prepass, -716:* -744 measured, and -745 in e1. It is as near as that because misses cancel. Reduce tiles came 2.27 us apart for f1T (1146.37 to 1216.67, 32 tiles), at 225 GB/s, and 2.18 for f2T, not 1.9: -318 with owT's instead of -340. Quantize tiles took 7.6 for f1T and 6.8 for f2T against 7.4, from 12.0 and 11.9 before: -306 instead of -282. That the load still waits for v4 was right: e7 took that wait away and gained 264. Under the first attention DVE's wait for scales fell from 73.7 to 10.3, for the exp from 50.6 to 21.4, and for the loads from 110.8 to 72.8, 131 in all; the attention ends 98 us earlier (887.4 and 788.9), against my 70.
- *Projections, +407:* 40 x (21.8 - 6.1 - 0.8) = +596. The place was right, and DVE's order too (e5b).
- *Weight loads, +195 and +98:* 6.35 us bare against 6.1. PE's waits for the matmuls of q and k, of v and g, and of the output projection were 13.6, 149.9 and 152.6 us before and are 112.9, 255.0 and 247.3 after: +299. e3 returned some 350, with f2T's and f1T's share (+29) in it. Right. The rows of before:

```profile
L1057 PE MATMUL ps<-a_xqf,a_wl 128*128 128x256 bf16 x1024 | 152.6, 320 | 13.6 <-DVE a_xqf L1019 13.6
...
L1076 PE MATMUL ps<-a_wl,a_xqf 128*128 128x512 bf16 x1024 | 302.8, 468 | 149.9 <-DMA a_wl<-q_vwT 68.0 <-DMA a_wl<-q_gwT 67.7 <-DVE a_xqf L1019 14.2
...
L1357 PE MATMUL ps<-a_oqf,a_wl 128*128 128x128 bf16 x2048 | 179.1, 273 | 152.6 <-DMA a_wl<-q_owT 139.0 <-DVE a_oqf L1338 13.6
```

- *Output quantization, +51:* 16 x (26.8 - 15.8) = +176.
- *Token tiles, +88:* 8 x (21.8 - 6.1) = +126.
- *_act_quant_fm and f2T's loads, +146 and +23:* (952.8 - 607.9) = +345.

Attention: 596 + 176 + 299 = 1,071, measured 1,085. Feed-forward: 126 + 345 = 471, measured 470. The forecast's sum was +298, so the miss between the spans is 514 us: P's size 48 x 4.7 + 16 x 5.1 + 4 x 27.7 = 418, the blocking 103, the loads and a rest without a name 21, and the prepass takes 28 back. The share of the blocking is worked out from the timeline; no run took it away by itself.

That the kernel pays for every microsecond of the chains is shown by e8: 998 us of chain, 990 to 1,030 measured. With the measured terms the break-even P would be an estimate of 2.36 - 812/912 = 1.47, where I had 1.57.

## What to carry to other kernels

Price an operation on an engine that has none in the trace by its kind, not by an average, and measure it first if all depends on it: on POOL the cast was cheap, the tensor_scalar dear, and a split scalar_tensor_tensor cost 5.2 us where DVE paid 1.2. Work given to a second engine helps only if its inputs are ready early in the first engine's order and if nothing, least of all a DMA issue, stands behind it. Here mending both would not have been enough: by adding e3's 350 and e5b's 230, an estimate that no run tested, some 1,000 of e2's 1,580 us would stay; by e6's prices that is POOL's own arithmetic. And a diff of two independent halves should be timed as two: here one gave 6% and the other took 12%.

## What the runs showed of the hardware

- POOL's tensor_scalar costs the same in bf16 and fp32, 2.77 us for 128x1024, and 3.70 with two operations; it is slower than POOL's own tensor_tensor (2.12), and DVE does it in 0.49 [rows 6]. So the correction of the rounding, two comparisons and two adds, is 10.4 us of the chain's 21.8.
- Side by side in e6, POOL's add and DVE's scalar_tensor_tensor both slow down. POOL's 12 took 34.2 us (32.5 busy, 1.7 of gaps); DVE's 20 took 44.5, of which some 8 ran alone at about 1.3. So some 12 pairs took 2.8 us each, where in turn the two take 3.1 and two gaps: sharing gained little.
- The output projection's 2 MB landed in 7.4 us on SP's queue in e3 and in 7.8 on POOL's [rows 9]. The queue itself hardly counted here (e9: 30 to 50 us); what stood ahead in it did (e3: 350).
